# Every third load of a weight ring moved from SyncE's DMA queue to GpSimd's

## What is computed

```python
xn = _layernorm(x)
# branch s: gated linear recurrence
q, v = xn @ Wq, xn @ Wv                    # 16 heads of 128
states[t] = lam * states[t-1] + v[t]       # scan over the sequence, lam = sigmoid(beta)
y = layernorm(q * states) * ln_g + ln_b
s = (y * silu(xn @ Wg)) @ Wo
# branch g: feed-forward with ternary weights and 8-bit activations
h = gelu(gelu(bitlinear158(xn, w1)))       # 2048 -> 8192
g = silu(bitlinear158(h, w2))              # 8192 -> 2048
out = x + s * g
```

## Time and profile before

| | us |
|---|---|
| median of 2 runs | 27270.2 (27267.11 to 27273.3) |
| the profiled execution | 27269.99 |
| its span on the slowest core (core 0) | 27268.4 |
| spans of the 8 cores | 27250.5 to 27268.4 |
| TensorE matmul busy | 16533.8 (61%) |
| VectorE busy | 3637.8 (13%) |
| ScalarE busy | 2165.6 (8%) |
| GpSimd busy | 275.9 (1%) |

### The profile page before, as it was taken

One profiled execution on the slowest core, in us unless ns is written; L12 is line 12 of the kernel. 1 busy time (PEld: TensorE's weight loads), 2 busy tenths in 40 slices (PEclk: granted clock), 3 DMA queues, 4 the chain that ended last, 5 costly groups with the idle time before them and its releaser, 6 DMA issues.

```text
span 27268.4 us, 132895 instructions; the slowest of 8 cores (27250.5 to 27268.4 us)
## 1 busy us (share of the span) xinstructions
PE 16533.8 (61%) x32774; PEld 3430.4 (13%) x32774; DVE 3637.8 (13%) x5534; ACT 2165.6 (8%) x4455; POOL 275.9 (1%) x526
## 2 busy tenths in 40 slices
PE   0133226776576766675667567675767566756676
PEld 0011001111111111111111111111111111111111
DVE  0144331000201110001000110101001100010001
ACT  2300320100100000000010010001000000000100
POOL 0000000000000000000000000000000000000000
DMA  7444331211121111111111112111211121111211
GB/s 174 167 124 125 59 56 65 83 60 36 71 80 66 40 66 69 70 53 50 70 70 66 46 60 88 59 38 73 71 71 43 59 71 68 58 44 71 74 65 39
DMA packets 742597, 1921.32 MB, mean 70 GB/s; under 512 B 401984, under 2 KB 418384, under 8 KB 623184
## 3 DMA queue, kind: packets, MB, share of 16 engines
q1 hardware_dynamic: 667920, 1476.57, 15.6%
q0 software_dynamic: 74048, 436.25, 5.9%
HBM read 1879.12 MB, written 134.22 MB: 74 GB/s over the span
## 4 chain that ended last, share of the span: by engine, by line
PE 62%; issue 19%; DVE 10%; DMA 5%; ACT 4%; DVEq 0%; ACTq 0%; SPq 0%; POOLq 0%; POOL 0%
PE psA L875 18%; PE psB L985 9%; PE psA L985 9%; PE psA L1153 6%; PE psA L1056 4%; PE psA L1080 4%; PE psA L1028 4%; PE psB L965 2%; PE psB L466 2%; DMA xping<-w 1%; DVE aB L971 1%; ACT sqd L522 1%; PE psB L834 1%; DMA prefb<-xpref 1%; DVE intscr L454 1%
## 5 line engine op out<-in xcount | busy, mean ns | idle before, releaser
L875 PE MATMUL psA<-wr,kfs 128*128 128x512 bf16 x8192 | 4778.4, 583 | 1268.9 <-PE psA L875 236.9
L985 PE MATMUL psA<-wr,aB 128*128 128x512 bf16 x4096 | 2389.2, 583 | 640.6 <-PE psA L985 89.5
L985 PE MATMUL psB<-wr,aB 128*128 128x512 bf16 x4096 | 2389.2, 583 | 618.8 <-PE psB L985 87.7
L1153 PE MATMUL psA<-wr,xnf 128*128 128x256 bf16 x4096 | 1516.9, 370 | 935.9 <-DVE xnf L1138 283.8
L466 PE MATMUL psB<-identsb,ktms 128*128 128x128 bf16 x2048 | 539.4, 263 | 2081.4 <-DVE ktms L458 1793.4
L965 PE MATMUL psB<-identsb,aA 128*128 128x128 bf16 x2048 | 541.3, 264 | 1880.0 <-DVE aA L955 1090.0
L875 PEld LDWEIGHTS psA<-wr,kfs 128*128 128x128 bf16 x8192 | 862.4, 105 | 5182.3 <-issue 5182.3
L898 DVE TENSOR_REDUCE st<-aA 128x1 f32<-128x8192 bf16 x32 | 278.0, 8686 | 9184.4 <-ACT aA L897 9182.7
L1028 PE MATMUL psA<-xnf,wr 128*128 128x512 bf16 x2048 | 1194.6, 583 | 337.1 <-PE psA L1028 63.1
L1080 PE MATMUL psA<-xnf,wr 128*128 128x512 bf16 x2048 | 1194.6, 583 | 319.3 <-PE psA L1080 59.8
L1056 PE MATMUL psA<-xnf,wr 128*128 128x512 bf16 x2048 | 1194.6, 583 | 307.3 <-PE psA L1056 56.3
(11 more groups left out here) (206 smaller groups left out, 6379.4 us busy)
## 6 DMA issues: line engine op xcount, KB each, us to landing
wr<-wq1t SPq DMA_DIRECT2D x512, 1024.0 KB, 5.0
wr<-wq2t SPq DMA_DIRECT2D x512, 1024.0 KB, 4.8
xping<-w POOLq DMA_DIRECT2D x256, 1024.0 KB, 5.2
xping<-x POOLq DMA_DIRECT2D x64, 1024.0 KB, 5.3
wr<-sqv SPq DMA_DIRECT2D x128, 512.0 KB, 3.3
wr<-sqq SPq DMA_DIRECT2D x128, 512.0 KB, 3.3
wr<-sqg SPq DMA_DIRECT2D x128, 512.0 KB, 3.3
wr<-sqo SPq DMA_DIRECT2D x64, 1024.0 KB, 4.8
```

Of the source, the lines that this page charges most:

```text
L875: tmm = T(lambda b, s_=slx, mm=m, icc=ic, i8=ic8, bk=bslot: b.matmul(bk, kfs[:, 512 * icc + 128 * mm:512 * icc + 128 * mm + 128], s_[:, 51 ...
L985: o_mm = T(lambda b, kcc=kc, mr_=mr, n_=n, s_=sl2, k_=kk, px=psX: b.matmul(px[:, 512 * n_:512 * n_ + 512], aB[:, 256 * kcc + 128 * mr_:256 ...
L1153: tmm = T(lambda b, s_=sl6, n_=n, mm=m, d_=dc, bk=wob: b.matmul(bk[:, 0:256], xnf[:, 512 * d_ + 128 * mm:512 * d_ + 128 * mm + 128], s_[:, ...
```

## The change

The ring's load function chooses the queue by the buffer: loads into buffer 2 (i%3 = 2) go out on GpSimd's queue, those into buffers 0 and 1 stay on SyncE's. Waits, semaphores, buffers and the order of emission stay as they are.

```diff
@@ -244,16 +244,17 @@
                 i = self.head
                 j = i % 3
                 src, w = self.srcs[i]
+                q = "gpsimd" if j == 2 else "sync"
                 if len(src.shape) == 3:
                     k3 = src.shape[1]
                     self.ready[j] = P.emit(
-                        "sync",
+                        q,
                         lambda b, s=wr[j], a=src, ww=w, kk=k3: b.dma_start(
                             out=s[:, 0:ww].rearrange("p (k j) -> p k j", k=kk), in_=a),
                         wait=self.free[j], inc=WRS[j], inc_n=16)
                 else:
                     self.ready[j] = P.emit(
-                        "sync",
+                        q,
                         lambda b, s=wr[j], a=src, ww=w: b.dma_start(out=s[:, 0:ww], in_=a),
                         wait=self.free[j], inc=WRS[j], inc_n=16)
```

## The result

| | median us | runs | lowest to highest |
|---|---|---|---|
| before | 27271.2 | 8 | 27261.3 to 27291.2 |
| after | 27417.7 | 9 | 27410.6 to 27429.8 |

The ratio is 1.0054, 95% interval 1.0043 to 1.0065: slower by 146 us, within 2%. The forecast was 27414. Each experiment further down stands beside the kernel before on its own chip, so the base moves a little (27244.6 to 27275).

A forecast was written before the change was run, and what follows sets the result against it. TensorE bounds the kernel, 61% busy, each matmul waiting for the one before, one every 0.73 us. 27270 + 128 (U on GpSimd) + 16 (V on GpSimd) = 27414 us; range 27340 to 27540.

The forecast's parts named there:

- U: FFN1 load of the next round's second half, released at a round's end, wanted at that next round's ninth matmul.
- V: FFN1 load of the first half of the round after next, released together with U, wanted 23 us later.
- 240 pairs in three thirds: FFN1's U and V pairs: 80 with U on GpSimd, 80 with V on GpSimd, 80 with both on SyncE, unchanged.
- U on GpSimd: 80 FFN1 pairs: U comes behind V and ends where V ends today, 1.6 us late each, 128 us.
- 6.02: Microseconds from the common release at an FFN1 round's end to the next round's ninth matmul, taken as U's deadline.
- rival 2: No cost in FFN1: U on GpSimd lands at 5.65, before 6.02; 27270, give or take 30; chance 0.10.
- The three V's: Three V loads read from the trace of FFN1, late by 1.9, 2.7 and 1.3 us against U's deadline.
- V on GpSimd: 80 FFN1 pairs: U on SyncE gets company from GpSimd, between 0 and 1.6 us, taken as 0.2 each, 16 us.
- Equal sharing: Rival for FFN1's pairs: each busy queue gets half, U late by 1.6 or 0.8 us; 192 us, 27462; chance 0.25.
- No cost: Same as rival 2: if two queues moved more than one, everything in FFN1 stays hidden; 27270; chance 0.10.
- More than the bytes: Rival: contention makes both kinds of FFN1 pair lose, 2.7 and 1.6 us; 344 us, 27614; more than 230 us: 0.15.
- GpSimd's other work: x loads at the residual and a pass's first ring loads queue behind others on GpSimd but stay hidden; counted 0.

The follow-up runs named there:

- e1_u80: Changed kernel, but only the 80 loads U with residue 2 go out on GpSimd, the other 410 buffer 2 loads stay on SyncE: 27399.7 us against 27244.6.
- e5_u240: Kernel before, but all 240 U's go out on GpSimd and every other ring load on SyncE: 27707.9 us against 27254.1, ratio 1.0166.
- e3_vlate: Changed kernel, but where U is on GpSimd, V on SyncE is held until the round's second matmul: 27243.2 us against 27244.6 for the kernel before.
- e2_rest: Changed kernel, but the 80 U's of buffer 2 stay on SyncE; all other buffer 2 loads on GpSimd: 27238.4 us against 27244.6 for the kernel before.
- e4_act: Changed kernel, but buffer 2 loads go out on ScalarE's queue instead of GpSimd's: 27445.0 us against 27244.6 for the kernel before, ratio 1.0075.
- e7_free_before: Kernel before, without the wait of each matmul for the one before it on TensorE: median 13942 us.
- e6_early: Changed kernel, but an FFN1 round's first chunk is given back after its last matmul, the 24th of 32: 27249.0 us against 27254.1 for the kernel before.
- e9_free_early: Kernel before, without the matmuls' wait for one another and with a round's first chunk given back after its last matmul: median 13270 us.
- e11_halves: Kernel before, without the matmuls' wait for one another; each FFN1 round does both row tiles with its first chunk, then both with its second: 12634, 12783 us.

## Why the prediction was right

**The bound and the place.** That no stage but FFN1 is touched, and there only the pairs of U and V, held: one row of waits on the ring, 80 times. The count of 240 pairs in three thirds held: 80 waits in the changed kernel, 81 in e1_u80, and three times the cost in e5_u240 (454 us). The granted clock of 1.00, which the prediction starts from, stands for a trace without clock records (see above); the sum does not use it.

**U on GpSimd, taken at 1.6, was 1.85.** The waits give 2.0 on average, of which 0.15 is idle time that the matmul has anyway; 80 x 1.85 = 148 against the 128 of the sum. The landing itself was forecast well: 7.51 after the release on average, 1.5 later than 6.02, with V first and U ending "where V ends today" (V's mean in the kernel before is 7.47). What the sum left out is the time from a landing to the matmul that waits for it, 0.35 us in nearly all of the 80. The 6.02 is when the matmul starts, so the landing is due at 5.67. The same 0.35 is missing elsewhere: a GpSimd load alone, taken as 0.37 in time, has about 0.06 to spare (e3_vlate), and rival 2 would have been decided there. The three V's that I had read, with a mean of 1.97, were slow ones: over the 240 pairs of the kernel before V's median landing is 7.35, 1.3 after 6.02, so I was right to go below them.

**V on GpSimd, taken at 0.2, was 0.** 16 us too much. The row I used, a load overtaken in a long queue at the turn of a pass, was no likeness of a load with its bytes already under way, and the company did not start 0.65 us behind, as written, but 3.1 (packets from 4.1 against 1.0); e2_rest has 0.5 us in a single wait. The two misses have opposite signs, 20 too little and 16 too much. So the last digits of 27414 are luck; the mechanism is not.

**The rivals.** Equal sharing, at 0.25, gave 27462, and is wrong for this change by e2_rest and e3_vlate. e4_act shows that sharing happens for loads 0.15 us apart. The Trainium skill (DMA: Bandwidth & Descriptors, Queues, rings and completion order) has each DMA engine take turns between queues, packet by packet; the measurements decide, and they show it only for loads that start almost together (4.8 becomes 6.3 at 0.15 us, and stays 4.8 at 0.46 and 0.7). "No cost" needed more rate from two queues than from one: the second load of a pair lands 7.37 us after the release on two queues and 7.35 on one (medians of the two traces), so there is none. With this agrees the other rule of the Trainium skill, that several issuing engines share one set of DMA engines (same page, Issuing engines are not separate DMA queues). "More than the bytes" does not appear.

**GpSimd's other work** cost nothing, as argued: e2_rest has all of it but the 80 U's, ring loads before x loads included, and stands at 0.9999.

## What to carry to other kernels

A load's lead is counted from what was released with it as much as from its own issue: moving one of two loads onto another queue added no rate here, it decided which came first, and the one that came second waited until the other was nearly through. So before spreading a ring over queues, look for the buffers given back in the same instant, put the most urgent load first and on the queue with the quickest issue, or give the buffers back apart. And where a kernel's most used engine sits at 60% busy in evenly spaced steps, question the steps before the loads. Time the steps of two widths against each other, too: that tells the clock where the clock record is missing.

## What the runs showed of the hardware

- A load of 1 MB issued 0.46 to 1.0 us after another one, on another queue, left the first one's landing unchanged (4.8 us on SyncE ahead of GpSimd's or ScalarE's, 5.1 on GpSimd ahead of SyncE's); issued 0.15 us after, it stretched it from 4.8 to 6.3.
- From the landing of a load to the start of the matmul that waits for it 0.35 us pass (changed kernel, 80 waits); in e7_free_before, without the matmuls' wait for one another, 0.24.
- Alone, U on GpSimd lands 5.6 us after its release (e3_vlate, e6_early), U on SyncE 4.9.
- ScalarE issues a load while its activation is still running, 0.15 us after SyncE's for the same release; GpSimd 0.46 us after SyncE's.
- A chain of 512-column matmuls in which each waits for the one before takes 0.73 us a matmul, without the wait 0.224; part of the difference is the clock. The view's 1.00 for the kernel before stands for a trace without clock records, and the columns went by at 1.2 GHz (0.213 us for 256). In e7_free_before the granted clock was 0.75 in FFN1, where TensorE sat idle in every round, in e9_free_early, with 4 tenths less of waiting, 0.90; it was 0.99 in the FFN2 behind it, and in e11_halves, with next to no waits, 0.99 in FFN1.
